# A conditional-logits kernel on one Trainium2 core: W_e's first two slices loaded singly, slice 0's high part in one operation, the bias product among tile 3's products, and W_u loaded behind the first quad's upper half

## What is computed

```python
# x [128, 128, 512], cond [128, 512], weight_matrix [1024, 512], W_proj [512, 512], b_proj [512]
u = gelu(cond @ W_proj + b_proj)                       # exact gelu
W_u, W_e = weight_matrix[:512], weight_matrix[512:]
out = x + (u @ W_u)[:, None, :] + einsum('bnd,dc->bnc', x, W_e)
```

## Time and profile before

| | us |
|---|---|
| median of 3 runs | 344.18 |
| lowest, highest | 343.98, 346.36 |
| the profiled execution: its time | 344.53 |
| the profiled execution: span of the trace | 342.4 |

### The profile page before, as it was taken

The page is one execution under the profiler, slowest core; times in us unless marked ns, Lnnn a source line. Parts: engine busy times, 40 slices in busy tenths (PEclk is TensorE's granted clock), DMA queues, the critical chain, the costliest instruction groups (busy, mean ns, idle before and its releaser), DMA issues.

```text
span 342.4 us, 7876 instructions
## 1 busy us (share of the span) xinstructions
PE 338.1 (99%) x2703; PEld 329.7 (96%) x2703; DVE 263.6 (77%) x302; ACT 249.1 (73%) x428; POOL 283.7 (83%) x203
## 2 busy tenths in 40 slices
PE   8999999999999999999999999999999999999996
PEld 4869999999999999999999999999999999999996
DVE  2989997777887777887777789777788877778811
ACT  3677787778777777877777877777787777787741
POOL 2499999988889898889898888989888888888860
PEclk9999999999999999999999999999999999999999
DMA  7998799878888977888997787898878799787216
GB/s 260 314 196 211 167 235 242 232 200 215 200 184 199 241 219 198 209 204 169 230 230 219 195 214 184 184 245 217 217 186 222 175 208 245 202 208 205 92 48 231
DMA packets 73353, 70.64 MB, mean 206 GB/s; under 512 B 2944, under 2 KB 68480, under 8 KB 69248
## 3 DMA queue, kind: packets, MB, share of 16 engines
q1 hardware_dynamic: 73344, 70.53, 81.5%
HBM read 36.96 MB, written 33.55 MB: 206 GB/s over the span
## 4 chain that ended last, share of the span: by engine, by line
PE 98%; DMA 1%; ACT 0%; issue 0%
PE banks L857 31%; PE banks L861 30%; PE banks L859 30%; PE banks L783 2%; PE banks L825 2%; PE banks L843 1%; DMA head_raw<-in_x 1%; PE banks L768 1%; PE banks L764 1%; PE banks L821 0%; PE banks L818 0%; PE banks L815 0%; ACT y L597 0%
## 5 line engine op out<-in xcount | busy, mean ns | idle before, releaser
L857 PE MATMUL banks<-t_hi,hi 128*128 128x256 f32 x496 | 140.6, 283 | 0.1
L861 PE MATMUL banks<-t_hi,lo 128*128 128x256 f32 x496 | 140.4, 283 | 0.0
L859 PE MATMUL banks<-t_lo,hi 128*128 128x256 f32 x496 | 140.4, 283 | 0.0
L857 PE MATMUL banks<-w_hi,hi 128*128 128x256 f32 x372 | 105.4, 283 | 0.0
L859 PE MATMUL banks<-w_lo,hi 128*128 128x256 f32 x372 | 105.3, 283 | 0.0
L861 PE MATMUL banks<-w_hi,lo 128*128 128x256 f32 x372 | 105.3, 283 | 0.0
L602 DVE STREAM_TRANSPOSE work<-quad_raw 128x1024 f32<-128x1024 f32 (+1 forms) x62 | 100.6, 1623 | 0.0
L857 PEld LDWEIGHTS banks<-t_hi,hi 128*128 128x128 f32 x496 | 95.2, 192 | 0.3 <-issue 0.2
L859 PEld LDWEIGHTS banks<-t_lo,hi 128*128 128x128 f32 x496 | 95.2, 192 | 0.0
L861 PEld LDWEIGHTS banks<-t_hi,lo 128*128 128x128 f32 x496 | 95.2, 192 | 0.0
L353 POOL TENSOR_TENSOR lo<-work,hi 128x1024 fp32r<-128x1024 f32 x31 | 75.0, 2418 | 16.9 <-ACT hi L454 16.9
(11 more groups left out here) (81 smaller groups left out, 411.4 us busy)
## 6 DMA issues: line engine op xcount, KB each, us to landing
out<-y SPq DMA_DIRECT2D x31, 1024.0 KB, 4.5
quad_raw<-in_x SPq DMA_DIRECT2D x120, 256.0 KB, 5.7
w_e<-in_L_cond_weight_matrix SPq DMA_DIRECT2D x2, 512.0 KB, 5.9
w_proj_sb<-in_L_cond_W_proj SPq DMA_DIRECT2D x2, 512.0 KB, 7.9
w_u<-in_L_cond_weight_matrix SPq DMA_DIRECT2D x1, 1024.0 KB, 8.5
quad_raw<-in_x SPq DMA_DIRECT2D x8, 128.0 KB, 8.1
out<-y SPq DMA_DIRECT2D x3, 256.0 KB, 2.2
head_raw<-in_x SPq DMA_DIRECT2D x1, 512.0 KB, 3.7
```

Source lines behind the costliest of these rows:

```text
L857: pe.matmul(psum[:, t, :], a_hi[:, 2 * j + t, :], b_hi[:, j, :], start=False, stop=False, skip_group_check=True)
L859: pe.matmul(psum[:, t, :], a_hi[:, 2 * j + t, :], b_lo[:, j, :], start=False, stop=False, skip_group_check=True)
L861: last = pe.matmul(psum[:, t, :], a_lo[:, 2 * j + t, :], b_hi[:, j, :], start=False, stop=(j == T - 1), skip_group_check=True)
```

## The change

On the loads: W_e's slices 0 and 1 come in a transfer of their own each, slices 2 and 3 in one; W_u is issued behind `load_first(0)`. On slice 0: POOL writes, at the start, a 128x512 tile that holds the identity where slice 0's diagonal lies (in the space of `bias`, which isn't used yet), and DVE forms slice 0's high part as slice plus that tile in one operation; slice 0's own diagonal is added later by POOL, once the high part is out. On PE: 2 dummies instead of 8 behind the transposes; another order among the first 24 products; cond's transposes later; and the bias product between tile 3's high-factor products and its low-factor products. On DVE and ACT: `sum_s3(0)` moves behind the first evacuation, and its high part `hi_s3(0)` into ACT's first period.

```diff
-WARM_ON = 8
+WARM_ON = 2
...
+        first_eye = bias[:, :]
...
             sp.dma_start(direct, x[:, 0:T, :]).then_inc(direct_loaded, 16)
-            for n in range(2):
-                load_w_e(n)
+            load_w_e(0, slice(0, 1))
+            load_w_e(1, slice(1, 2))
+            load_w_e(2, slice(2, NJ))
...
+            load_first(0)
             sp.dma_start(w_u[:, :, :], w_u_dram).then_inc(w_u_loaded, 16)
-            load_first(0)
             load_first(1)
...
+            pool.memset(first_eye, 0.0).then_inc(first_eye_zeroed, 1)
+            pool.wait_ge(first_eye_zeroed, 1)
+            pool.affine_select(out=first_eye, in_=first_eye, compare_op=ALU.not_equal, fill=1.0,
+                               base=0, pattern=[[-1, C]], channel_multiplier=NJ).then_inc(first_eye_ready, 1)
...
-            for j in range(1, NJ):
-                pool.wait_ge(w_e_loaded[j // 2], 16)
...
+            pool.wait_ge(w_e_loaded[1], 16)
+            add_ident(1, w_diag_ready)
+            pool.wait_ge(w_hi_ready[0], 1)
+            add_ident(0, first_diag_ready)
+            pool.wait_ge(w_e_loaded[2], 16)
+            for j in range(2, NJ):
+                add_ident(j, w_diag_ready)
...
-            dve.wait_ge(ident_ready, 1)
+            dve.wait_ge(first_eye_ready, 1)
             dve.wait_ge(w_e_loaded[0], 16)
-            first_diag = diagonal(0)
-            dve.tensor_tensor(first_diag, first_diag, ident[:, :], ALU.add).then_inc(first_diag_ready, 1)
-            dve.wait_ge(first_diag_ready, 1)
-            dve.tensor_copy(w_hi[:, 0, :], w_e[:, 0, :]).then_inc(w_hi_ready[0], 1)
+            dve.tensor_tensor(w_hi[:, 0, :], w_e[:, 0, :], first_eye, ALU.add).then_inc(w_hi_ready[0], 1)
             split_direct(0)
             split_direct(1)
+            dve.wait_ge(first_diag_ready, 1)
...
             sum_s1(0, 0, True)
-            sum_s3(0, 0, True)
...
             evacuate(0, slice(0, 1))
+            sum_s3(0, 0, True)
             evacuate(0, slice(1, T))
...
             high(0)
+            low(0, 0)
+            high(1)
+            low(0, 1)
+            for j in range(1, NJ):
+                for t in range(T):
+                    low(j, t)
+                if j == NJ - 1:
+                    pe.wait_ge(cond_loaded, 16)
+                    flip(flip_psum, by_j(cond_sb[:, :]), cond_flipped)
+                low_w(j - 1)
                 if j + 1 < NJ:
                     high(j + 1)
+            low_w(NJ - 1, last=True).then_inc(multiplied, 1)
...
+            pe.wait_ge(direct_hi_ready, HEAD)
+            for j in range(NJ):
+                second_product(1, x_hi[1], w_hi, j, first=(j == 0))
+                second_product(1, x_hi[1], w_lo, j)
+
             pe.wait_ge(w_u_loaded, 16)
             pe.wait_ge(u_ready, 1)
...
             pe.wait_ge(direct_lo_ready, HEAD)
             for j in range(NJ):
-                second_product(1, x_hi[1], w_hi, j, first=(j == 0))
-                second_product(1, x_hi[1], w_lo, j)
                 last = second_product(1, x_lo[1], w_hi, j, last=(j == NJ - 1))
```

More of the change, by code:

```diff
@@ L151, in build_cond_residual @@
         b_proj_loaded = sem("b_proj_loaded")
-        w_e_loaded = [sem(f"w_e_loaded{n}") for n in range(2)]
+        w_e_loaded = [sem(f"w_e_loaded{n}") for n in range(3)]
         direct_loaded = sem("direct_loaded")
@@ L177, in build_cond_residual @@
         w_diag_ready = sem("w_diag_ready")
+        first_eye_zeroed = sem("first_eye_zeroed")
+        first_eye_ready = sem("first_eye_ready")
         first_diag_ready = sem("first_diag_ready")
@@ L259, in load_quad, with load_w_e @@
                                  x_dram[q, :, :, bass.ds(HEAD + k * QUAD, QUAD), :]).then_inc(quad_loaded[p], 16)
-            def load_w_e(n):
-                sp.dma_start(w_e[:, 2 * n:2 * n + 2, :], w_e_dram[:, 2 * n:2 * n + 2, :]).then_inc(w_e_loaded[n], 16)
+            def load_w_e(n, slices):
+                sp.dma_start(w_e[:, slices, :], w_e_dram[:, slices, :]).then_inc(w_e_loaded[n], 16)
             sp.dma_start(direct, x[:, 0:T, :]).then_inc(direct_loaded, 16)
-            for n in range(2):
-                load_w_e(n)
+            load_w_e(0, slice(0, 1))
+            load_w_e(1, slice(1, 2))
+            load_w_e(2, slice(2, NJ))
             sp.dma_start(cond_sb[:, :], cond).then_inc(cond_loaded, 16)
@@ L324, in _, with add_ident @@
                                base=0, pattern=[[-1, P]], channel_multiplier=1).then_inc(ident_ready, 1)
+            pool.memset(first_eye, 0.0).then_inc(first_eye_zeroed, 1)
+            pool.wait_ge(first_eye_zeroed, 1)
+            pool.affine_select(out=first_eye, in_=first_eye, compare_op=ALU.not_equal, fill=1.0,
+                               base=0, pattern=[[-1, C]], channel_multiplier=NJ).then_inc(first_eye_ready, 1)
             pool.wait_ge(ident_ready, 1)
-            for j in range(1, NJ):
-                pool.wait_ge(w_e_loaded[j // 2], 16)
+            def add_ident(j, done):
                 diag = diagonal(j)
-                pool.tensor_tensor(diag, diag, ident[:, :], ALU.add).then_inc(w_diag_ready, 1)
+                pool.tensor_tensor(diag, diag, ident[:, :], ALU.add).then_inc(done, 1)
+            pool.wait_ge(w_e_loaded[1], 16)
[5 more added lines that the diff above has]
+                add_ident(j, w_diag_ready)
             def split_t(n):
@@ L534, in period @@
                 if early:
+                    hi_s3(k, p, True)
                     snap_c(k, p, first)
@@ L570, in _ @@
             hi_s2(0, 0, True)
-            hi_s3(0, 0, True)
             period(0, 0, True, True)
@@ L790, in high, with low, low_w @@
                     product(t, x_hi[0], w_hi, j, first=(j == 0))
-            high(0)
-            for j in range(NJ + 1):
+            def low(j, t):
+                if j == 0:
+                    pe.wait_ge(direct_lo_ready, t + 1)
+                product(t, x_lo[0], w_hi, j)
+            def low_w(j, last=False):
+                pe.wait_ge(w_lo_ready[j], 1)
+                for t in range(T):
+                    end = product(t, x_hi[0], w_lo, j, last=last)
+                return end
+            high(0)
+            low(0, 0)
+            high(1)
+            low(0, 1)
+            for j in range(1, NJ):
+                for t in range(T):
+                    low(j, t)
[3 more added lines that the diff above has]
+                low_w(j - 1)
                 if j + 1 < NJ:
                     high(j + 1)
[L797 to L809, removed]
+            low_w(NJ - 1, last=True).then_inc(multiplied, 1)
             pe.wait_ge(cond_hi_ready, 1)
```

## The result

| | before | after |
|---|---|---|
| median of 7 runs each, us | 344.86 | 348.37 |
| lowest, highest | 343.98, 346.73 | 347.74, 349.33 |
| profiled execution: its time | 344.53 | 349.33 |
| profiled execution: span | 342.4 | 347.0 |

The ratio is 1.0092, with a 95% interval of 1.0067 to 1.0118: the changed kernel is some 3.2 us slower. The forecast was 345.4, with 343.9 to 346.4 for 8 in 10; the measured median lies 2.0 us above that range. A part of that is the base: the forecast counted from a median of 344.18, and these runs of the kernel before have 344.86. Change against change it is 1.2 us forecast and 3.2 us measured. It is slower, as forecast, and the size is wrong.

What follows compares the result with a forecast made beforehand. PE holds 98% of the chain, but DVE, without slack, sets M5 of quad 1. Bias copy 0.58 late plus S3's 0.60 is 1.18; 344.53 + 1.18 = 345.71, for the median 345.4 us, 8 in 10 from 343.9 to 346.4.

Steps and rivals of the forecast that it cites:

- The step that failed: Loads at the start: slice 1 lands at 6.6 as before, and a smaller transfer pays no visible extra.
- cond's 0.65: Loads: cond's 256 KB land 0.65 behind W_e's second half, a like share of the 1.35 between 512 KB halves.
- stand in a full queue: nothing: Loads of cond, W_proj, tiles 2 and 3: issued 0.43 later, but at no cost.
- The rival about this step: Loads: each transfer takes 1.35 whatever its size, so slice 1 lands at 7.95; 346.7 us, 8 in 100.
- The bias product 8 products later: PE, quad 0: it starts at 21.22, the seed ends at 25.56, DVE's bias copy starts 0.58 late at 25.61.
- S3's 0.60: DVE, quad 0: S3, formerly done in spare time, is paid behind the first evacuation, 0.60 more.
- The forecast's 1.18: DVE up to M5 of quad 1: 0.58 plus 0.60 arrive there in full, so M5 starts at 37.73.
- The gain of the start, 0.50: PE's head: the fourth product starts at 8.16 instead of 8.66, a gain of 0.50, bounds 0.07 and 1.13.
- W_u behind the upper half: Loads: W_u issued after the upper half instead of before it changes nothing either way.
- PE keeping its gain: Rival at M5 of quad 1: DVE does not hold PE, so 0.50 and 0.18 go through; 343.5 us, all or part 22 in 100.
- The clock: Rival on the clock, 5 in 100; only it and unnamed things reach past 340.7 to 347.6.

Runs made afterwards that it cites:

- E1: Kernel before with only W_e's first half split, slices 0 and 1 each loaded singly: 346.96 us, ratio 1.0071.
- E13: Kernel before with W_e loaded as slices 0 and 2, then 1 and 3, in rows of 2 KB: 346.62 us, ratio 1.0046.
- E12: Kernel before with cond loaded in two transfers of 64 partitions each: 345.69 us, ratio 1.0033.
- E10: Kernel before with W_proj in one transfer of 1 MB instead of two of 512 KB: 345.56 us, ratio 1.0019.
- E3: Kernel before with the bias product among tile 3's products and S3 of quad 0 behind the first evacuation: 346.06 us, ratio 1.0042.
- E2: Changed kernel with W_e loaded in two halves again, all else as changed: 346.27 us, ratio 1.0043.
- E6: Kernel before with only S3 of quad 0 behind the first evacuation and its high part in ACT's first period: 344.62 us, ratio 1.0000.
- E7: Kernel before with only the bias product moved behind eight of tile 3's products: 345.53 us, ratio 1.0023.
- E5: Changed kernel with W_e in halves and the bias product, S3 and its high part in their old places: 344.76 us, ratio 1.0000.
- E4: Changed kernel with W_u issued ahead of the upper half again: 348.19 us, ratio 1.0103.
- E11: Kernel before with W_e's slices 0 and 1 loaded singly and W_proj in one transfer: 347.63 us, ratio 1.0099.
- E9: Kernel before with W_e's slices 2 and 3 loaded singly, 0 and 1 together: 348.77 us, ratio 1.0107.
- E8: Kernel before with W_e's first half cut by partitions into two transfers of 256 KB, rows of 4 KB kept: 346.25 us, ratio 1.0055.

## Why the prediction was wrong, step by step

**The step that failed** is that about the transfers. The prediction let slice 1 land "at 6.6 as before, since the bytes ahead of it are the same", took cond's 0.65 as proof that "a smaller transfer pays no visible extra here", and of cond, W_proj and tiles 2 and 3 said that they "stand in a full queue: nothing". Slice 1 landed at 7.2, slices 2 and 3 at 9.6, and the lower half 4.70 late. Equal bytes were taken for equal time. The price of the split, alone in an otherwise unchanged kernel, is 2.4 us (E1). cond was a poor witness: its 256 KB are one piece of memory, where a slice is 128 pieces of 2 KB with gaps of 6 KB between them, and E13 shows that this matters by itself; and even cond, cut in two, costs 1.1 us (E12). The rival about this step (each transfer takes its 1.35, 346.7, 8 in 100) had the right place and sign, but looked only at slice 1's own landing and not at what comes behind it in the queue. Slice 1 came 0.6 late and not 1.35, and one transfer fewer, in E10, let the lower half land no earlier (22.3 against 21.5).

**The bias product 8 products later: right.** E3 has each of its times within 0.15 us. E2 has them too, in the changed kernel with W_e in halves: the bias copy at 26.22 behind 1.33 us of waiting for the seed, forecast 25.61. The 0.6 between them is the bias product at 21.93 instead of 21.22, and of that 0.55 is the start's missing gain (the fourth product at 8.71 instead of 8.16).

**S3's 0.60: right**, with the condition that E6 and E7 make plain: it counts because the seed is late.

**In the changed kernel itself this chain doesn't bind.** Its seed ends at 28.04 + 0.57 = 28.61, before DVE is ready for the bias copy at 29.07, and DVE doesn't wait for it:

```profile
28.04 0.57 ACT L513 COPY banks<-banks 128x512 f32<-128x512 f32 x1 [2.91 <-PE banks L873]
```

So S3 behind the copy costs nothing there either, as in E6: the copy is earlier by as much as S3 is later, and from the lower half to M5 of quad 1 it is 14.93 us with S3 moved and 14.97 with S3 in its old place (E1). The late lower half has taken the place of the late seed; whichever of the two is later counts, not their sum. That is why the parts don't add up: 2.4 (E1) and 1.5 (E3) make 3.9, and the whole is 3.2. That the whole lies above E1 at all I can't explain from these traces; the landings scatter from one execution to the next, and only one of each kernel is traced. The forecast's 1.18 thus holds for the kernel with W_e in halves, but for the missing gain of the start; in the traced execution of the changed kernel it is no part of the loss. That the direction came out as forecast is owed to another cause than the one it was forecast from.

**The gain of the start, 0.50, was mis-sized.** It is 0.04 in the changed kernel, through slice 1's later landing, and 0.22 with W_e in halves (E5), through POOL's slower addition. As the prediction says, it passes nowhere, since DVE's chain to M5 of quad 1 sets the end: E5 is at 1.0000.

**W_u behind the upper half: nothing** that shows, as said (E4 against after, and E5, which has it and is at 1.0000). **PE keeping its gain** was excluded by every kernel with the new start. **The clock**, to which the forecast gave 5 in 100, did not fall in after, whose seven executions have a mean of 0.999 or 1.000, though PE stands idle for 0.94 us before its first product and for 0.29, 0.43, 1.48 and 1.09 later:

```profile
6.00:42.00 36.00, 31.30 (x169) 1.00 0.96 225
```

One trace has a fall: in E13, with all 8 dummies, idle times of 0.67 and 2.09 close behind one another were followed by a granted clock of 0.50. Its price there is about 1.5 us, the estimate from the 3 us at 0.50. That the clock could take this kernel past 347.6 is shown by no run.

## What to carry to other kernels

Where a kernel starts behind a full queue of loads, a change to one of the first transfers can change the landing of those that follow (E1: the lower half at 25.4 instead of 21.5), and the one to look at is the last that the bounding engine needs, not the one that was split. Equal bytes were not equal time here (the lower half has the same bytes ahead of it and lands at 26.2 instead of 21.5): read the windows' GB/s and the landings of a run with the new transfers before anything is rested on them. And before a producer is moved later, look for work that fills the consumer's wait; moving both, as with the bias product and S3 in E3, paid twice (1.5 us, of which 0.8 or 0.9 and 0.6 or 0.7), where no later landing covered it. When several changes delay the same engine, compare the waits in one trace before their times are added: here the later one counted, not the sum.

## What the runs showed of the hardware

- W_e's slices in rows of 2 KB with gaps make the queue drop to 139 to 266 GB/s for some 2 us when they are served, against 266 to 416 in the same windows before the change. In all such kernels but E11 the 16 shares of W_u then land 3.2 to 4.1 us apart instead of 1.1, and the lower half is 3.0 to 4.7 us late (E13, E4, E1, E9, after). Whether the gaps or the mere number of pieces does it, why the shares stay apart, and why E11 is spared, is open: no row names a cause, and no run has contiguous pieces of 2 KB in place of W_e's.
- One load cut by partitions into two of 64, with unchanged rows, costs 1.1 us (E12) and 1.6 to 1.9 us (E8). One transfer fewer (E10) gives nothing. No run has one more transfer over all 128 partitions with unchanged rows.
- With such loads the runs of one kernel scatter more: 345.7 to 349.1 (E1) against 343.9 to 344.9 for the kernel before beside it. A part of that is the clock: the slowest of E1, E8, E11 and E13 have a mean granted clock of 0.994 or 0.995.
- TensorE's granted clock fell from 1.00 to 0.50 for some 3 us behind idle times of 0.67 and 2.09 us (E13); it stayed at 1.00 through idle times of 0.94, 0.29, 0.43, 1.48 and 1.09 us (after).
- A POOL addition of 128x128 took 1.03 and 0.98 us beside a DVE operation of 128x512 that reads two SBUF tiles (E5), 0.52 and 0.53 beside one that reads PSUM and SBUF (E5, after), and 0.52 while DVE was idle (after, from 10.18).
